# Second expert projection in float32r parts, weight split on GpSimd, ends of the expert stage rearranged

## What is computed

```python
xn = _layernorm(x, axis=-1)
x = x + attention(xn, ...) + moe_forward(xn, ...)
# attention: 32 query heads of 8 features over 8 key/value heads, softmax over 512 tokens,
#            and a memory term elu(q) @ memory / (elu(q) @ memory_norm), mixed by a sigmoid
# moe_forward:
logits = x @ router_w                                   # 8 experts, the best two of each token
for e in range(E):                                      # w1[e] 256 x 1024, w2[e] 512 x 256
    f1 = permuted * mask @ w1[e]
    g, u = jnp.split(f1, 2, axis=-1)
    act = jax.nn.silu(g) * u
    out = out + jnp.where(mask, act @ w2[e], 0.0)
shared = jax.nn.silu(x @ w_gate) * (x @ w_up) @ w_down  # hidden width 1024
```

## Time and profile before

| | us |
|---|---|
| runs (three) | 773.37, 775.11, 775.14; median 775.11 |
| profiled execution, time | 772.37 |
| profiled execution, span | 770.6 |
| TensorE busy in the span | 707.3 |
| VectorE, ScalarE, GpSimd busy | 586.9, 487.0, 132.5 |
| attention, about | 146 to 492 |
| expert tiles, about | 495 to 694 |
| late shared stage, about | 697 to 766 |

### The profile page before, as it was taken

One profiled execution on the slowest core, in us unless ns is written; L12 is line 12 of the kernel. 1 busy time (PEld: TensorE's weight loads), 2 busy tenths in 40 slices (PEclk: granted clock), 3 DMA queues, 4 the chain that ended last, 5 costly groups with the idle time before them and its releaser, 6 DMA issues.

```text
span 770.6 us, 14200 instructions
## 1 busy us (share of the span) xinstructions
PE 707.3 (92%) x3976; PEld 373.9 (49%) x3977; DVE 586.9 (76%) x800; ACT 487.0 (63%) x886; POOL 132.5 (17%) x282
## 2 busy tenths in 40 slices
PE   5999999799889888998998888799999999998997
PEld 2456544522222222221222212388888888887886
DVE  5375588799999889899999984378777777756764
ACT  2472600388888888888888878656656665646321
POOL 1000000756531111011111111000000000005730
PEclk9999999999999999999999999999999999999999
DMA  9729100177411111011110172041111111122420
GB/s 316 246 68 328 44 1 0 47 234 235 130 48 32 32 32 32 17 32 32 32 32 24 38 262 90 15 151 44 51 54 49 46 54 54 54 90 81 143 92 28
DMA packets 49951, 65.35 MB, mean 85 GB/s; under 512 B 8168, under 2 KB 42880, under 8 KB 49920
## 3 DMA queue, kind: packets, MB, share of 16 engines
q1 hardware_dynamic: 38848, 40.85, 16.7%
q10 hardware_dynamic: 8000, 15.73, 6.2%
q0 software_dynamic: 3072, 8.39, 3.5%
HBM read 40.15 MB, written 24.38 MB: 84 GB/s over the span
## 4 chain that ended last, share of the span: by engine, by line
PE 76%; ACT 10%; issue 5%; DVE 5%; POOL 1%; DMA 1%; ACTq 1%; SPq 0%; DVEq 0%; POOLq 0%
PE ps L1386 14%; PE ps L1357 14%; ACT att L729 9%; PE ps L1410 9%; PE ps L1456 9%; PE ps L1238 7%; PE ps L1488 6%; DVE smax L993 3%; PE ps L1230 3%; PE ps L1503 3%; PE ps L1447 2%; PE ps L1198 2%; PE ps L1263 2%; PE ps L1346 1%; POOL acc L557 1%
## 5 line engine op out<-in xcount | busy, mean ns | idle before, releaser
L993 DVE TENSOR_REDUCE smax<-ps 128x2 f32<-128x1024 f32 x256 | 302.5, 1221 | 36.3 <-PE ps L1263 33.2
L729 ACT ACTIVATE att<-ps 128x512 f32<-128x512 f32 x512 | 267.7, 602 | 54.6 <-PE ps L1410 51.8
L1410 PE MATMUL ps<-att 51*128 51x512 bf16 x512 | 165.8, 384 | 32.8 <-ACT att L729 19.3
L1263 PE MATMUL ps<-att 48*128 48x512 bf16 x512 | 163.5, 386 | 1.4 <-DVE smax L993 1.4
L1357 PE MATMUL ps<-att,v_head 128*32 128x512 f32 x1024 | 137.1, 608 | 1.7 <-ACT o_sb L688 0.6
L1410 PEld LDWEIGHTS ps<-att 51*128 51x128 bf16 x512 | 39.7, 93 | 201.6 <-ACT att L729 95.8
L1386 PE MATMUL ps<-att_r 128*128 128x512 f32 x456 | 117.5, 406 | 3.1 <-DVE att_r L1054 1.6
L1050 DVE TENSOR_TENSOR att_r<-big,att_r 128x1024 fp32r<-128x1024 f32 x76 | 89.8, 1222 | 23.9 <-ACT att_r L709 23.8
L1386 PEld LDWEIGHTS ps<-att_r 128*128 128x128 f32 x456 | 85.5, 188 | 21.4 <-DVE att_r L1054 2.1
L709 ACT ACTIVATE att_r<-big 128x1024 fp32r x74 | 74.3, 1051 | 19.0 <-issue 19.0
L1456 PE MATMUL ps<-big,xn 128*128 x312 | 73.7, 380 | 0.0
(11 more groups left out here) (164 smaller groups left out, 691.1 us busy)
## 6 DMA issues: line engine op xcount, KB each, us to landing
big<-w ACTq DMA_DIRECT2D x8, 1024.0 KB
q_stacks<-big SPq DMA_DIRECT2D x12, 512.0 KB
att<-q_stacks SPq DMA_DIRECT2D x64, 96.0 KB, 2.1
slot_x<-zeros SPq DMA_DIRECT2D x1, 4992.0 KB, 17.2
e_x<-slot_x SPq DMA_DIRECT2D x39, 128.0 KB, 2.0
slot_y<-xn SPq DMA_DIRECT2D x39, 128.0 KB, 1.7
big<-w ACTq DMA_DIRECT2D x8, 512.0 KB
att<-k_stacks SPq DMA_DIRECT2D x64, 48.0 KB, 2.0
```

What stands on the lines that cost most here:

```text
L729: act.activation(probs[:, t % 2, g, :], ps[:, RING[turn_of(u) % 3], :], ACT.Exp, scale=SCALE)\
L993: dve.reduce_max(smax[:, s % 2, :].rearrange("p (half v) -> p half v", half=2)[:, :, v], ps[:, bank:bank + 2, :], X_AXIS).then_inc(max_don ...
L1263: return pe.matmul(ps[:, bank + half, :], q_st[s][rows, g, P * st:P * (st + 1)], k_st[s][rows, :], start=True, stop=True)
L1410: pe.matmul(ps[:, RING[turn % 3], :], k_st[s][rows, P * t:P * (t + 1)], q_st[s][rows, g, :], start=True, stop=True).then_inc(scores_ready, 1)
```

## The change

The second projection becomes a product in float32r parts, 12 matmuls of 128x128 by 128x256 in place of 4 float32 ones. ScalarE's new `round_hT` rounds h's transpose out of PSUM, VectorE's `rest_hT` takes `copy_hT`'s place. w2's parts are made on GpSimd by the new `parts_w2`: a copy of 128x1024 into `e_v_hi`, an operation on one element, and a subtraction of 128x1024 into `e_v_lo`; it waits for `down(j - 2)`, which last read these buffers. They lie in xnT for even tiles, in o_sb and v_all for odd ones. The late weights all go to att now: gate and up are asked for at tile 38, down at tile 39, all by ScalarE's queue. `split_x(0)` and `low_x(0)` move to tile 39, `split_w(0)` to its end, `split_w(1)` to tile 40.

At the front of the experts the last pair's transposition moves behind `up(1)`, into bank 7; its copy on ScalarE behind `round_w1(2)`, `finish_o` to the end of VectorE's tile 1, `add_o` to GpSimd's tile 1, and TensorE waits for the copy at tile 3. On GpSimd `split_max(1, 1)` stands ahead of the additions of the memory term. At the end `split_down` signals each of its last four banks, VectorE adds each as it is done, and two of the last four stores go out on ScalarE's queue. The router's weights move into big.

```diff
-        wu_late = xnT[:, :, 0:FS]
-        wd_late = [v_all[:, 4 * f:4 * f + 4, :].rearrange("p c n -> p (c n)") for f in range(4)] + \
-                  [o_sb[:, f // 2, D * (f % 2):D * (f % 2 + 1)] for f in range(4)]
+        wu_late = att[:, 4864:6912].rearrange("p (k n) -> p k n", k=KD)
+        wd_late = [att[:, 2560 + D * f:2560 + D * (f + 1)] for f in range(FS // P)]
...
-        e_hT = xnf[:, 2560:3584].rearrange("p (a k n) -> p a k n", a=2, k=F // P)
+        e_hT_hi = xn_r[:, 2560:3584].rearrange("p (a n) -> p a n", a=2)
+
+        e_v_hi = [xnT_r[:, 0, 0:1024], o_sb_r[:, :]]
+        e_v_lo = [xnT_r[:, 1, 0:1024], v_all_r[:, :]]
...
-            for c in range(NT - 4, NT):
+            for c in range(NT - 4, NT, 2):
                 sp.wait_ge(s_mix, NT * TOPK)
                 sp.wait_ge(s_add, c + 1)
                 sp.dma_start(out_rows[c * P:(c + 1) * P, :], acc[:, c, :]).then_inc(stored, 16)
-            sp.wait_ge(stored, 16 * (3 + 4))
+            sp.wait_ge(stored, 16 * (3 + 2))
+            sp.wait_ge(stored_act, 16 * 2)
...
             split_max(0, 0)
             stage_v(0, 0, 0, 0)
+            split_max(1, 1)
...
-            add_o(PAIRS - 1, 1, BATCH - 1, H - 2)
+            def parts_w2(j, a):
+
+                e = pool.value_load(expert[0:1, bass.ds(j, 1)], min_val=0, max_val=E - 1)
+                w = w2_sb[:, bass.ds(e, 1), :, :].rearrange("p o k n -> p (o k n)")
+                wait(pool, y_in_psum, j - 1)
+                pool.tensor_copy(e_v_hi[a], w).then_inc(ev_hi_ready, 1)
+                pool.wait_ge(ev_hi_ready, j + 1)
+                pool.tensor_tensor(max_rest[0:1, 0:1], zeros[0:1, 0:1], zeros[0:1, 0:1], ALU.add)
+                pool.tensor_tensor(e_v_lo[a], w, e_v_hi[a], ALU.subtract).then_inc(ev_lo_ready, 1)
+
+            def tile(j, pair, a):
+                if isinstance(j, int) and j == 0:
+                    pool.wait_ge(experts_known, 1)
+                    pool.wait_ge(w12_loaded, 16 * 2 * E)
+                if isinstance(j, int) and j == 1:
+                    add_o(PAIRS - 1, 1, BATCH - 1, H - 2)
+                    pool.wait_ge(oT_in_psum, PAIRS)
+                if live(j):
+                    parts_w2(j, a)
+            over_tiles(pool, tile)
...
-            copy_oT(PAIRS - 1, 1)
-
-
-
-            def load_shared():
-                act.wait_ge(pv_done, ST * STEPS)
-                act.dma_start(wu_late, w_up.rearrange("(k p) n -> p k n", p=P)).then_inc(shw_loaded, 16)
-                act.dma_start(v_all[:, :, :].rearrange("p (f c) n -> p f (c n)", f=4),
-                              w_down[0:4 * P, :].rearrange("(f p) n -> p f n", p=P)).then_inc(shw_loaded, 16)
-                act.dma_start(o_sb[:, :, :].rearrange("p a (f n) -> p (a f) n", n=D),
-                              w_down[4 * P:8 * P, :].rearrange("(f p) n -> p f n", p=P)).then_inc(shw_loaded, 16)
-
-            def load_gate():
+
+
+
+            def load_gate_up():
 
                 act.wait_ge(up_done, 2 * (TILES - 1))
                 act.dma_start(wg_late, w_gate.rearrange("(k p) n -> p k n", p=P)).then_inc(shw_loaded, 16)
+                act.dma_start(wu_late, w_up.rearrange("(k p) n -> p k n", p=P)).then_inc(shw_loaded, 16)
+
+            def load_down():
+                act.wait_ge(up_done, 2 * TILES)
+                act.dma_start(att[:, 2560:4608].rearrange("p (f n) -> p f n", n=D),
+                              w_down.rearrange("(f p) n -> p f n", p=P)).then_inc(shd_loaded, 16)
...
+            def round_hT(j, a):
+                act.wait_ge(hT_in_psum, j + 1)
+                wait(act, y_in_psum, j - 1)
+                act.activation(e_hT_hi[:, a, :], ps[:, 3, :], ACT.Copy).then_inc(hT_hi_ready, 1)
...
+                if isinstance(j, int) and j == 1:
+                    copy_oT(PAIRS - 1, 1, LAST_OUT)
+                if isinstance(j, int) and j == TILES - 1:
+                    load_gate_up()
+                if isinstance(j, int) and j == TILES:
+
+                    load_down()
+                    split_x(0)
                 if live(j - 3):
...
+                if live(j - 1):
+                    round_hT(j - 1, 1 - a)
+                if isinstance(j, int) and j == TILES:
+                    act.wait_ge(shw_loaded, 80)
                     split_w(0)
                 if isinstance(j, int) and j == TILES + 1:
+                    split_w(1)
                     copy_y(j - 2, pair - 1, a)
-                if isinstance(j, int) and j == 3:
-                    load_shared()
             over_tiles(act, tile)
 
 
-            split_w(1)
             for m in range(LAST):
                 act.wait_ge(s_up, 2 * (FIRST + m) + 1)
                 act.wait_ge(s_h, FIRST + max(m - 1, 0))
...
+            for c in range(NT - 3, NT, 2):
+                act.wait_ge(s_mix, NT * TOPK)
+                act.wait_ge(s_add, c + 1)
+                act.dma_start(out_rows[c * P:(c + 1) * P, :], acc[:, c, :]).then_inc(stored_act, 16)
...
-            def copy_hT(j, a):
-                dve.wait_ge(hT_in_psum, j + 1)
-                wait(dve, y_in_psum, j - 1)
-                dve.tensor_copy(e_hT[:, a, :, :].rearrange("p k n -> p (k n)"), ps[:, 3, :]).then_inc(hT_ready, 1)
+            def rest_hT(j, a):
+                dve.wait_ge(hT_hi_ready, j + 1)
+                dve.tensor_tensor(e_hT_lo[:, a, :], ps[:, 3, :], e_hT_hi[:, a, :], ALU.subtract).then_inc(hT_lo_ready, 1)
...
+                    low_x(0)
                 if live(j - 1):
-                    copy_hT(j - 1, 1 - a)
+                    rest_hT(j - 1, 1 - a)
+                if isinstance(j, int) and j == 1:
+                    finish_o(PAIRS - 1, 1)
...
-            add_shared(3)
+            for c in range(4):
+                dve.wait_ge(last_down, c + 1)
+                row = row_of(NT - 4 + c)
+                dve.tensor_tensor(row, row, ps[:, 4 + c, 0:D], ALU.add).then_inc(s_add, 1)
...
-                e = pe.value_load(expert[0:1, bass.ds(j, 1)], min_val=0, max_val=E - 1)
-                pe.wait_ge(hT_ready, j + 1)
+                pe.wait_ge(hT_lo_ready, j + 1)
+                pe.wait_ge(ev_lo_ready, j + 1)
                 wait(pe, y_ready, j - 1)
-                for k in range(F // P):
-                    w = w2_sb[:, bass.ds(e, 1), k, :].rearrange("p o n -> p (o n)")
-                    last = pe.matmul(ps[:, 6 + a, 0:D], e_hT[:, a, k, :], w, start=k == 0, stop=k == F // P - 1)
+                for count, (hs, ws) in enumerate(((e_hT_hi, e_v_hi), (e_hT_lo, e_v_hi), (e_hT_hi, e_v_lo))):
+                    for k in range(F // P):
+                        last = pe.matmul(ps[:, 6 + a, 0:D], hs[:, a, P * k:P * (k + 1)], ws[a][:, D * k:D * (k + 1)],
+                                         start=count == 0 and k == 0, stop=count == 2 and k == F // P - 1)
...
+                    transpose_o(PAIRS - 1, 1, LAST_OUT)
+                if isinstance(j, int) and j == 3:
+                    pe.wait_ge(oT_copied, PAIRS)
...
-            transpose_o(PAIRS - 1, 1)
-            pe.wait_ge(oT_copied, PAIRS)
...
-                last.then_inc(s_hused, 1)
+                    if m == LAST - 1:
+                        last.then_inc(last_down, 1)
+                if m < LAST - 1:
+                    last.then_inc(s_hused, 1)
```

More of the change, by code:

```diff
@@ L569, in steps @@
                     i = blk * 4 + s
+                    if not (first and s < 2):
+                        split_max(i, s)
                     if not (first and s == 0):
-                        split_max(i, s)
                         stage_v(i, b, h0 + s, s)
```

45 lines of the change are left out of this document (27 added, 18 removed).

## The result

The changed kernel takes **829.15 us** (median of 6 runs, 827.01 to 830.4) against 774.24 for the kernel before beside it (6 runs, 772.56 to 775.14): ratio 1.0707 [1.069, 1.0724]. It is slower, as forecast, but by 55 us where the prediction had 28, and outside its range. The profiled execution has a span of 826.9 us (before 770.6), so 56.3 us are to be found in the trace.

What follows compares the result with a forecast made beforehand. TensorE bounds the kernel now, VectorE and GpSimd excluding each other would bound the changed tile; -1.7 - 1.1 + 32.2 - 0.4 - 1.0 = +28.0 on 772.4 gives 800.4, for the median 803, range 768 to 822.

Steps and rivals of the forecast that it cites:

- The mechanism: Expert tiles: VectorE two-input SBUF instructions and GpSimd SBUF reads exclude each other both ways; chance 0.70, 791 to 820.
- unhindered work: Rival, expert tiles: GpSimd works beside VectorE unhindered, tile 5.05 us, total 766.7; chance 0.16.
- GpSimd alone waiting: Rival, expert tiles: only GpSimd waits, VectorE does not; total 767 to 783, most likely 769; chance 0.14.
- The durations: GpSimd's w2 operations in each expert tile: copy 1.02 us, small operation 0.30, subtraction 2.35, together 3.7.
- The dear copy: GpSimd's w2 copy at the two-input rate, 2.2 us; the tile would be 7.2 us, +75 in all.
- the tile, 6.03 us: Expert stage, 36 tiles: 6.03 us a tile instead of 5.135, +32.2 us.
- the five operations follow one another: Each expert tile in series: VectorE 1.18, copy 1.02, VectorE 1.18, small one 0.30, subtraction 2.35, sum 6.03 us.
- Second projection on TensorE: Expert tiles: 12 float32r matmuls take 1.54 us instead of 1.63, gain 0.09 a tile, at most 3.1 in 36.
- Front of the experts: Before tile 2: ScalarE's work comes 1.2 us sooner, so tile 2 gains 1.1 us (0 to 1.5).
- Start of attention: TensorE's 2.41 us wait for split_max at 150.00 goes away: -1.7 us (0 to -2.4).
- End of the experts: From the last up, U: split weight ready U + 7.1, last down done U + 8.7; gain 0.4 us (-1 to 1.5).
- The tail: After the last matmul: one addition instead of four, stores on two queues, -1.0 us (0 to -1.5).

Runs made afterwards that it cites:

- experiment 1: Changed kernel with GpSimd's copy and subtraction of w2 replaced by memsets that only write zeros: 758.32 us, ratio 0.9797 to the kernel before.
- experiment 3: Changed kernel plus 18 needless small matmuls filling TensorE's idle time in every second tile of the loop: 810.36 us, ratio 1.0457 to the kernel before.
- Experiment 2: Changed kernel with GpSimd's subtraction replaced by a second copy of w2: 774.37 us, ratio 1.0001 to the kernel before.
- experiment 5: Changed kernel with the w2 copy moved to ScalarE, GpSimd only subtracting, without the one-element operation: 758.14 us, ratio 0.9796 to the kernel before.
- experiment 8: Kernel before with only split_max(1, 1) moved ahead of GpSimd's additions: 770.91 us against 774.01, ratio 0.9957.
- experiment 4: Changed kernel with the second projection as it was before, all other parts kept: 769.30 us, ratio 0.9941 to the kernel before.

## Why the prediction was right in kind and wrong in size

**The mechanism held, both halves.** The rows of before showed only GpSimd waiting for VectorE; that VectorE waits too was an assumption, with the larger share of the chances. It is now measured: L1102 goes from 1.22 us for one to 2.31 in the mean, and back when GpSimd only writes (experiment 1). That is what the Trainium skill, SBUF — State Buffer, "Who interferes with whom", states, and here it is worth 71 us. The two rivals, unhindered work and GpSimd alone waiting, are both out. The first would also have been mispriced: with nothing in the way the total is 758, not 767, mostly since the tile without waits is 4.80 us.

**The durations held.** Copy 1.04 (1.02), subtraction 2.37 (2.35), from rows of other sizes. The dear copy of 2.2 us is out. The small operation takes 0.18 us when nothing is in its way.

**The term that failed is the tile, 6.03 us, measured 6.87.** The miss of 0.84 us, 30.4 in 36 tiles, has three parts.
- *The clock, 0.65 us a tile, some 21 us in 32 tiles.* The prediction foresaw TensorE's gap and priced it as the gap alone. Behind the gaps of 2.1 us in every second tile the clock fell, and `up` took 4.2 to 4.6 us instead of 2.91. With the gap filled the tile is 6.15 us instead of 6.80, and the kernel 19 us faster (experiment 3). Of the 0.85 us a tile by which `up` is longer, about 0.2 was covered by VectorE's work.
- *The order of the work, 0.12 us a tile, some 4 us.* That this part is so small is partly luck. The sum had the copy and the small operation (1.32 us) in the series and VectorE's other 1.7 us under GpSimd's long subtraction. The timeline shows the reverse: `make_h`, `rest_x` and `rest_hT` run beside the short copy, and the subtraction (604.05 in experiment 3, 610.05 in the changed kernel) starts 0.3 us before `rest_w1` and meets it nearly whole. VectorE's own 4.04 us and 2.1 of waiting make 6.15. Experiment 2 misses for the same reason, 5.32 for 4.6, and experiment 5 shows the opposite order, where the subtraction costs `rest_w1` 0.08 us an operation (mean 1.30 against 1.22).
- *The first four tiles, some 6 us.* Tiles 2 to 5 take 29.86 us, 7.46 each. TensorE waits 2.78 and 4.07 us there, and the `up`s behind take 4.59 and 5.27. In the longer of the two waits VectorE's pair takes 7.34 us:

```profile
505.80 7.34 DVE L1102 TENSOR_TENSOR att_r<-big,att_r 128x1024 fp32r<-128x1024 f32 x2 [0.36 <-ACT att_r L750]
```

Its second operation begins at 508.63 and takes 4.51 us, longer than any that was forecast (up to 3.5): GpSimd's subtraction (508.71 to 511.07) and the next tile's copy (511.03 to 512.06) both run before it. So an engine that waits is not always served next, which "the five operations follow one another" had taken for granted.

"Five operations in a row" was thus the right bound but not the picture: GpSimd stands for 4.53 us in every pair of tiles, waiting for `down` to free its buffer. My signs for it being right (TensorE idle about 1 us a tile, operations of up to 3.5 us) came out, as (247.43 - 207.95)/36 = 1.1 us a tile and a longest operation of 3.55 in the regular tiles (600 to 615); "GpSimd near full" did not, with 159.05 of 247.43 us. The range's upper end, 822, was named as the top of the main case, which by its own bounds was 820; both are under the result.

**Second projection on TensorE.** Predicted 0.09 us less, in truth 0.34: the twelve loads take 1.39 us, start to start, in experiment 1, where 1.54 was read from the earlier trace rows, and `up` behind them is shorter too. (The sign named, 12 loads in 1.61 us, came out as 1.47, 606.30 to 607.77 in the changed kernel.) Here it is lost in the waits, in experiment 5 it is the gain.

**Front of the experts.** `up` of tile 2 came 1.2 us sooner as predicted, but nothing of it stayed. From the changed kernel's timeline:

```profile
498.55 4.59 PE L1440 MATMUL ps<-att_r 128*128 128x512 f32 x12 [2.78 <-DVE att_r L1106]
```

Tile 1 starts 3.7 us earlier than before, so the wait for the parts of w1 grows to 2.78 us (1.59 in the earlier trace rows), and the slow clock behind it makes `up` 4.59 us instead of 3.02. At tile 3, counted from the last weighted values, the changed kernel is 0.3 us behind the one before. "Whatever tile 1 gains is spent waiting" was right; that the waiting has a price of its own was missed.

**Start of attention.** -1.65 in the trace for -1.7, -3.1 in the runs of the edit alone. The trace and the medians differ by more than the interval. The trace of experiment 8 has the same gain as that of the changed kernel, 1.6 us from the reduction at 133.41 (there 135.13) to tile 1's `up` (495.25, there 495.38), but the code ahead of that reduction, untouched, ran 1.7 us longer in it, and the clock fell at other places, so that its span is only 0.4 us shorter. One trace a kernel can't say what the rest of the 3.1 is; it stays open.

**End of the experts.** -0.8 for -0.4, with the chain that was described:

```profile
751.01 1.04 POOL L612 CAST xnT_r<-big 128x1024 fp32r x1 [2.52 <-PE ps L1510]
751.04 2.09 DVE L1170 TENSOR_TENSOR split<-xnT,split 128x1024 fp32r<-128x1024 f32 x1 [0.26 <-ACT split L811]
...
753.14 2.33 POOL L615 TENSOR_TENSOR xnT_r<-big,xnT_r 128x1024 fp32r<-128x1024 f32 x1
...
755.54 0.54 PEld L1510 LDWEIGHTS ps<-xnT_r,xn_r 128*128 128x128 f32 x4 [2.76 <-issue]
```

With U = 748.60, the last weights' parts are ready at U + 6.9 (predicted 7.1) and the late stream starts at U + 8.35 (8.7). The low part of x did get in between, and took 2.09 us instead of 1.22.

**Late stage and tail.** The late stage gained 1.5 us that no step of the prediction had. Before, its first 4 us ran at a clock of 0.59, behind a gap of 2.06 us; after, at 1.00 throughout (the windows above). This is not shown to come from the change: experiment 8, with the late stage of before, had 1.00, and experiment 4, with that of the changed kernel, had 0.60. The tail gained 2.0 instead of 1.0: stores of 1.00 and 1.04 us on two queues took the place of one series of 1.80, and I had taken the additions alone as the path. How the 2.0 splits between additions and stores was not tried.

## What to carry to other kernels

Before work goes to GpSimd because it stands idle, look at what VectorE does at that moment: a GpSimd instruction that reads SBUF and a VectorE one with two SBUF inputs cost the sum of both, while GpSimd's writes ran beside such an operation at no cost, and its reads beside VectorE work with one input in PSUM. Where such work must be there, its place counts as much as its length: copy and subtraction behind `down` cost some 70 us, the subtraction alone, released by ScalarE's copy at a moment of PSUM work on VectorE, nearly nothing (758.1 us, the best version here, 8.6% under the changed kernel); how much of that is the place and how much the missing copy was not tried apart. And a wait on the busy engine is to be priced with the clock behind it: in the changed kernel's loop each gap of 2.1 us was followed by an `up` that took up to 1.7 us more.
